# Gated cross-attention stack on one Trainium2 core: query projection and VectorE's rotation of it one step sooner in each batch of the first attention

## The chip, the cores and the metric

The kernel runs on one core of one Trainium2 chip. A core has TensorE (PE in the profile: matmuls, with weight loads shown apart as PEld), VectorE (DVE), ScalarE (ACT), GpSimd (POOL) and SyncE (SP, which here only issues transfers). The metric is the time of one execution in microseconds (us); lower is better.

## The reference

The program is four layers of attention and feed-forward over x, 16 batches of 128 rows and 256 columns, float32. The change touches the first attention of layer 0 alone. There the 128 rows of a batch are channels and the 256 columns are positions:

```
q = einsum('oc,bct->bot', Wq, layernorm(x)) + bq     # 16 heads of 8
k = einsum('oc,bct->bot', Wk, ctx) + bk              # 4 key heads of 8
v = einsum('oc,bct->bot', Wv, ctx) + bv
q = q * cos + rotate_half(q) * sin
k = k * cos + rotate_half(k) * sin
scores = einsum('bhqd,bhkd->bhqk', q, k) * scale     # 16 heads, 256 x 256
attn = softmax(scores, axis=-1)
out = einsum('bhqk,bhkd->bhqd', attn, v)
x = x + tanh(g) * (einsum('oc,bct->bot', Wo, out) + bo)
```

## The kernel before

Every engine runs a list of instructions written out by hand, and takes them in that order; semaphores tie the lists together. In the first attention (`l0_attention`) the lists of TensorE, VectorE, ScalarE and GpSimd all come from one loop over u = 0 to 127. Each u is a step; b = u // 8 is the batch and i = u % 8 the step in it, so a batch has 8 steps, called step 0 to step 7 below.

**What stands in every step.** TensorE computes a tile of scores (`pe_scores`, line 352, two matmuls into one of two score banks), then the scores of another batch once more with the row maximum taken off (`pe_shifted_scores`, line 374), then a second tile of scores. VectorE takes the row maximum of each tile of scores (`dve_max`, line 539), two per step. ScalarE takes the exponential of the shifted scores (`act_exp`, line 678). The maxima run 24 tiles (a batch and a half) ahead of the exponentials. A tile of scores may be written only when the maximum of the tile two before it has been taken:

```
pe.wait_ge(*maxed.at(v - 1))
```

**What stands in some steps.** These carry the batch b - 1 to its end and prepare the batch b + 3:

- Step 0: TensorE weighs the values with the exponentials, first half (`pe_weigh`, line 389, 16 matmuls); GpSimd normalises x of batch b + 3 (`pool_norm`, line 756), which the query projection reads.
- Step 1: TensorE turns the weighed values (`pe_turn_av`, line 397) and turns the context of batch b + 3 (lines 315, 316), which ScalarE copies (line 645); VectorE divides by the sums (`dve_normalise`, lines 562, 567).
- Step 2: TensorE weighs the second half (line 389 again).
- Step 3: TensorE turns it (line 397) and projects the queries of batch b + 3 (`pe_queries`, lines 322 and 323). VectorE splits the maxima of the batch b + 1 into three bfloat16 parts (`dve_split_top`, lines 547 to 553), divides (lines 562, 567) and rotates the queries (`dve_rope_queries`, lines 508 and 509, which read the bank of the projection). GpSimd adds the two halves of the rotation (line 761).
- Step 4: TensorE turns the split maxima (`pe_turn_top`, line 363), into the bank that the queries were in, so it waits for the split and for line 509:

```
pe.wait_ge(*top_split.at(b + 1))
...
elif b + 2 < NB:
    pe.wait_ge(*q_read.at(b + 3))
```

- Step 5: TensorE turns the outputs (line 403) and projects the keys (`pe_keys`, lines 330 and 331); VectorE rotates the keys (lines 519 and 520).
- Step 6: output projection (line 408), values of the context (lines 338 and 339), which VectorE copies with the bias (line 532).

The steps for batch b + 3 exist for b = 0 to 12, 13 times; the ones for b - 1 from b = 1. The query parts go to memory and come back as the stack that `pe_scores` of batch b + 3 reads, a batch and a half later.

Of the kernel before, what the change touches and what calls it, by code (L numbers as in the profile page):

```python
# [234 lines left out]
def l0_attention(m, l1):  # L235
# [75 lines left out]
    def pe_turn_context(b):  # L311
        pe.wait_ge(*ctx_in[b % 3].at(16 * (b // 3 + 1)))
        if b >= 3:
            pe.wait_ge(*v_ready.at(b))
        pe.transpose(k_bank(b)[:, 0:P], ctx_t[b % 3][:, 0:P], m.ident)
        pe.transpose(k_bank(b)[:, P:2 * P], ctx_t[b % 3][:, P:2 * P], m.ident).then_inc(*ctx_turned.up())

    def pe_queries(b):
        if b >= 3:
            pe.wait_ge(*ctx_kept.at(b + 1))  # L320
        pe.wait_ge(*xn_ready.at(b + 1))
        pe.matmul(q_bank(b)[:, 0:T0], wq, xn_t[b % 3], start=True, stop=True)
        pe.matmul(q_bank(b)[:, T0:2 * T0], wqp, xn_t[b % 3], start=True, stop=True).then_inc(*q_made.up())

    def pe_keys(b):
        if b >= 3:
            pe.wait_ge(*top_kept.at(b - 1))
        else:
            pe.wait_ge(*ctx_kept.at(b + 1))
        pe.matmul(k_bank(b)[0:32, 0:T0], wk[:, 0:32], ctx_t[b % 3], start=True, stop=True)  # L330
        pe.matmul(k_bank(b)[0:32, T0:2 * T0], wk[:, 32:64], ctx_t[b % 3], start=True, stop=True).then_inc(*k_made.up())

    def pe_values_of_context(b):
        if b >= 3:
            pe.wait_ge(*k_read.at(b + 1))
        else:
            pe.wait_ge(*q_read.at(b + 1))
        pe.matmul(q_bank(b)[:, 0:32], ctx_t[b % 3][:, 0:P], wv, start=True, stop=True)
        pe.matmul(q_bank(b)[:, 32:64], ctx_t[b % 3][:, P:2 * P], wv, start=True, stop=True).then_inc(*v_made.up())

    def pe_scores(v):
        b, hp, c = v // 16, v // 2 % 8, v % 2
        if v % 16 == 0:
            pe.wait_ge(*q_in[b % 3].at(16 * (b // 3 + 1)))
            pe.wait_ge(*k_in[b % 3].at(16 * (b // 3 + 1)))
        if v >= 2:
            pe.wait_ge(*maxed.at(v - 1))
        q3 = q_stack[b % 3].rearrange("p (h t) -> p h t", h=H0)
        k3 = k_stack[b % 3].rearrange("p (g t) -> p g t", g=G0)
        for j in range(2):  # L350
            h = 2 * hp + j
            last = pe.matmul(score_bank[v % 2][:, j * T0:(j + 1) * T0], q3[0:STACK + 48, h, c * P:(c + 1) * P], k3[0:STACK + 48, h // 4, :], start=True, stop=True)  # L352
        last.then_inc(*scored.up())

    def pe_turn_top(b):
        pe.wait_ge(*top_split.at(b + 1))
        if b == 0:
            pe.wait_ge(*v_ready.at(3))
        elif b + 2 < NB:
            pe.wait_ge(*q_read.at(b + 3))  # L360
        else:
            pe.wait_ge(*top_kept.at(b))
        pe.transpose(pro_bank.bitcast(BF16)[0:96, 0:P], top_part[b % 2], m.ident_bf).then_inc(*top_turned.up())
# [29 lines left out]
    def pe_turn_av(b, jp):  # L393
        n = 2 * b + jp
        pe.wait_ge(*av_kept.at(n + 1))
        for i in range(4):
            last = pe.transpose(av_bank[:, i * P:(i + 1) * P], av_t[jp][:, i * P:(i + 1) * P], m.ident)
        last.then_inc(*av_turned.up())
# [11 lines left out]
    def pe_program():  # L410
        pe_turn_context(0)
        pe.wait_ge(*w.q_loaded.now())
        pe_queries(0)
        pe.wait_ge(*w.k_loaded.now())
        pe_keys(0)
        pe_turn_context(1)
        pe_queries(1)
        pe_values_of_context(0)
        pe_keys(1)
        pe_turn_context(2)  # L420
        pe_queries(2)
        pe_values_of_context(1)
        pe_keys(2)
        pe_values_of_context(2)
        pe.wait_ge(*w.late.now())
        pe.wait_ge(*m.set_act.now())
        for v in range(AHEAD):
            pe_scores(v)
            if v == 16:
                pe_turn_top(0)  # L430
        for u in range(LAST):
            b, i = divmod(u, 8)
            v = 2 * u + AHEAD
            if v < NV:
                pe_scores(v)
            pe_shifted_scores(u)
            if v + 1 < NV:
                pe_scores(v + 1)
            if b >= 1:
                if i == 0:  # L440
                    pe_weigh(b - 1, 0)
                if i == 1:
                    pe_turn_av(b - 1, 0)
                if i == 2:
                    pe_weigh(b - 1, 1)
                if i == 3:
                    pe_turn_av(b - 1, 1)
                if i == 5:
                    pe_turn_out(b - 1)
                if i == 6:  # L450
                    pe_project(b - 1)
            if i == 4 and b + 1 < NB:
                pe_turn_top(b + 1)
            if b + 3 < NB:
                if i == 1:
                    pe_turn_context(b + 3)
                if i == 3:
                    pe_queries(b + 3)
                if i == 5:
                    pe_keys(b + 3)  # L460
                if i == 6:
                    pe_values_of_context(b + 3)
            if u == LAST - 8:
                pe.wait_ge(*m.l0f_weights.loaded.now())
            if u in (LAST - 8, LAST - 7):
                ffn.pe_turn_x(0, u - (LAST - 8))
            if u == LAST - 6:
                ffn.pe_router(0)
        last = NB - 1
        pe_weigh(last, 0)  # L470
        pe.wait_ge(*exped.at(LAST))
        ffn.pe_up(0)
        pe_turn_av(last, 0)
        pe_weigh(last, 1)
        ffn.pe_up(1)
        pe_turn_av(last, 1)
        pe_turn_out(last)
        pe_project(last)
# [91 lines left out]
    def dve_program():  # L570
        ffn.dve_clear()
        dve_clear_stack(0)
        dve_clear_stack(1)
        dve_clear_stack(2)
        dve_clear_values()
        for b in range(3):
            dve_norm_stats(b)
        for b in range(3):
            dve_norm(b)
        dve.wait_ge(*w.q_loaded.now())  # L580
        dve_rope_queries(0)
        dve.wait_ge(*w.k_loaded.now())
        dve_rope_keys(0)
        dve.wait_ge(*cleared.now())
        dve_rope_queries(1)
        dve_values(0)
        dve_rope_keys(1)
        dve_rope_queries(2)
        dve_values(1)
        dve_rope_keys(2)  # L590
        dve_values(2)
        dve.wait_ge(*m.set_act.now())
        dve.wait_ge(*w.late.now())
        dve.tensor_tensor(bo[:, 1:2], bo[:, 0:1], m.gates[:, 0:1], ALU.mult).then_inc(*cleared.up())
        for v in range(AHEAD):
            dve_max(v)
            if v == 15:
                dve_split_top(0)
        for u in range(LAST):
            b, i = divmod(u, 8)  # L600
            v = 2 * u + AHEAD
            if v < NV:
                dve_max(v)
            if v + 1 < NV:
                dve_max(v + 1)
            if i == 3 and b + 1 < NB:
                dve_split_top(b + 1)
            if b >= 1:
                if i == 1:
                    dve_normalise(b - 1, 0)  # L610
                if i == 3:
                    dve_normalise(b - 1, 1)
            if b + 3 < NB:
                if i == 0:
                    dve_norm_stats(b + 3)
                if i == 3:
                    dve_rope_queries(b + 3)
                if i == 5:
                    dve_rope_keys(b + 3)
                if i == 6:  # L620
                    dve_values(b + 3)
            if u == LAST - 12:
                for n in (0, 1):
                    dve.wait_ge(*q_out[n].now())
                    dve.wait_ge(*k_out[n].now())
                ffn.dve_set()
            if u == LAST - 11:
                ffn.dve_norm_stats(0)
            if u == LAST - 9:
                ffn.dve_norm(0)  # L630
            if u == LAST - 5:
                ffn.dve_router_logits(0)
            if u == LAST - 4:
                ffn.dve_router_top(0)
                ffn.dve_router_pick(0)
        dve_normalise(NB - 1, 0)
        ffn.dve_gate(0)
        dve_normalise(NB - 1, 1)
        ffn.dve_gate(1)
# [3890 lines left out]
```

## Time and profile before

| | |
|---|---|
| median of 3 runs | 1953.11 us (1948.66 to 1958.79) |
| profiled execution | 1949.41 us, its span 1948.1 us |
| busy: TensorE, VectorE, ScalarE, GpSimd | 87%, 68%, 49%, 41% of the span |
| mean granted clock of TensorE | 0.955 of full speed |
| VectorE row maxima, line 539 | 256, together 164.5 us |
| first attention, batches b = 1 to 12 | 58.69 to 263.56 us, about 17.07 us each |

An engine that is busy 87% of the span isn't busy so in every stage. What a change in one stage is worth is read from that stage: from the chain of work that ended last, and from what each engine waited for there.

### The profile page before, as it was taken

The page shows a single profiled execution, that of the slowest core. Times are in us where ns is not written, and L with a number is a line of the kernel's source. Part 1 is how long each engine was busy: PE and PEld are TensorE (multiplying, and loading weights), DVE is VectorE, ACT ScalarE, POOL GpSimd, SP SyncE. Part 2 cuts the span into 40 slices and gives each one's busy share as a digit, 9 for nine tenths or more (in the row PEclk, how much of TensorE's full clock was granted, in tenths as well). Part 3 has the DMA queues.
Part 4 walks back from the last instruction along what each step waited for, and adds up shares of the span by engine and source line. Part 5 has one row for each costly group of instructions (what it writes and reads, how often), then busy time and mean ns, then how long its engine had stood idle before and what let it go on. Part 6 is the DMA issues. An engine that isn't in the chain of part 4 may idle for free.

```text
span 1948.1 us, 35947 instructions
## 1 busy us (share of the span) xinstructions
PE 1702.4 (87%) x12191; PEld 1178.0 (60%) x12221; DVE 1327.5 (68%) x4195; ACT 945.2 (49%) x2227; POOL 789.6 (41%) x957
## 2 busy tenths in 40 slices
PE   6999988979897988989896787788999999987898
PEld 2444444646666777777684555456777777765445
DVE  7888874523466887887747888864667677667446
ACT  2767673213323777777544555334444444443352
POOL 3333321266654656664525454220143433343340
PEclk7999999989997999999898999799999999989898
DMA  4454422048843333443213543019010000031857
GB/s 110 103 124 104 97 54 90 23 157 304 287 138 84 85 88 84 95 84 68 74 37 102 154 120 82 17 37 322 1 36 19 33 10 1 13 98 37 240 192 307
DMA packets 180437, 200.41 MB, mean 103 GB/s; under 512 B 86500, under 2 KB 150129, under 8 KB 176928
## 3 DMA queue, kind: packets, MB, share of 16 engines
q1 hardware_dynamic: 164224, 156.32, 29.4%
q0 software_dynamic: 15168, 41.54, 6.2%
q8 instruction: 99, 1.62, 0.4%
q14 instruction: 82, 0.67, 0.1%
q10 hardware_dynamic: 864, 0.26, 0.1%
HBM read 131.88 MB, written 75.44 MB: 106 GB/s over the span
## 4 chain that ended last, share of the span: by engine, by line
PE 51%; DVE 24%; ACT 8%; issue 8%; POOL 4%; DMA 4%; SPq 1%; another core or an unknown queue 0%; DVEq 0%; ACTq 0%; POOLq 0%
PE psum L1058 4%; PE psum L3474 3%; PE psum L3400 3%; DVE sbuf L539 3%; PE psum L389 3%; PE psum L3449 2%; PE psum L352 2%; PE psum L3467 2%; PE psum L1337 2%; ACT sbuf L3837 2%; PE psum L2286 2%; PE psum L1070 2%; PE psum L1356 1%; PE psum L1702 1%; PE psum L4057 1%
## 5 line engine op out<-in xcount | busy, mean ns | idle before, releaser
L539 DVE TENSOR_REDUCE sbuf<-psum 128x2 f32<-128x512 f32 x256 | 164.5, 684 | 35.3 <-PE psum L352 34.2
L190 POOL TENSOR_TENSOR sbuf<-sbuf 128x1 f32<-128x1 f32 x128 | 73.2, 574 | 276.5 <-DVE sbuf L182 276.4
L2021 ACT ACTIVATE sbuf<-psum 128x512 f32<-128x512 f32 x256 | 137.8, 592 | 69.6 <-PE psum L1772 68.4
L3837 ACT ACTIVATE sbuf<-psum,sbuf 128x128 f32<-128x128 f32 x256 | 113.6, 455 | 89.8 <-DVE sbuf L3649 89.5
L678 ACT ACTIVATE sbuf<-psum 128x1024 f32<-128x1024 f32 x128 | 131.1, 1025 | 47.5 <-PE psum L374 43.1
L3929 POOL DMA_INDIRECT l_slot_inputs<-sbuf x96 | 97.0, 1011 | 102.0 <-DVE sbuf L3720 76.7
L3474 PE MATMUL psum<-sbuf 128*128 128x256 f32 x512 | 124.2, 386 | 4.9 <-DVE sbuf L3667 4.9
L352 PE MATMUL psum<-sbuf 112*128 112x256 bf16 x512 | 104.2, 288 | 16.3 <-DVE sbuf L539 11.2
L3400 PE MATMUL psum<-sbuf 128*128 128x256 f32 x512 | 117.0, 382 | 0.8 <-ACT sbuf L3801 0.8
L1897 DVE CUSTOM_DVE_ANT_0 sbuf<-psum,sbuf 128x128 f32<-128x128 f32 x512 | 112.6, 285 | 0.3 <-PE psum L1751 0.3
L3400 PEld LDWEIGHTS psum<-sbuf 128*128 128x128 f32 x512 | 97.1, 192 | 20.6 <-issue 8.6
L3474 PEld LDWEIGHTS psum<-sbuf 128*128 128x128 f32 x512 | 93.6, 193 | 16.1 <-issue 5.8
L352 PEld LDWEIGHTS psum<-sbuf 112*128 112x128 bf16 x512 | 41.8, 100 | 94.1 <-DVE sbuf L539 56.5
L1905 DVE TENSOR_REDUCE sbuf<-psum 128x8 f32<-128x1024 f32 x64 | 77.5, 1212 | 31.0 <-PE psum L1763 31.0
L1058 PE MATMUL psum<-sbuf 128*128 128x512 f32 (+1 forms) x192 | 86.7, 595 | 0.0
L2013 ACT ACTIVATE sbuf<-sbuf 128x128 f32<-128x128 f32 x256 | 81.3, 397 | 0.0
L3845 ACT ACTIVATE sbuf<-psum 128x512 f32<-128x512 f32 x64 | 38.4, 600 | 87.7 <-PE psum L3457 87.3
L3607 DVE COPY sbuf<-psum 128x1024 f32<-128x1024 f32 x32 | 39.2, 1224 | 60.3 <-ACT sbuf L3808 44.2
L3467 PE MATMUL psum<-sbuf 128*128 128x512 f32 x128 | 69.5, 625 | 9.8 <-ACT sbuf L3845 9.8
L3449 PEld LDWEIGHTS psum<-sbuf 128*128 128x128 f32 x512 | 67.3, 199 | 17.3 <-issue 15.1
L1772 PE MATMUL psum<-sbuf 128*128 128x128 f32 x512 | 68.5, 276 | 6.0 <-ACT sbuf L2021 5.8
L374 PE MATMUL psum<-sbuf 128*128 128x512 bf16 x226 | 70.7, 383 | 3.1 <-DMA sbuf<-sbuf 1.1
(436 smaller groups left out, 4474.0 us busy)
## 6 DMA issues: line engine op xcount, KB each, us to landing
l_pair_outputs<-sbuf SPq DMA_DIRECT2D x24, 512.0 KB, 7.1
sbuf<-in_l_gu_pairs SPq DMA_DIRECT2D x32, 384.0 KB, 8.1
sbuf<-l_pair_outputs SPq DMA_DIRECT2D x16, 768.0 KB, 15.9
sbuf<-l_q_parts SPq DMA_DIRECT2D x16, 384.0 KB
l_q_parts<-sbuf SPq DMA_DIRECT2D x64, 96.0 KB, 2.2
sbuf<-l_q_parts SPq DMA_DIRECT2D x32, 192.0 KB
l_k_parts<-sbuf SPq DMA_DIRECT2D x64, 96.0 KB, 2.1
sbuf<-l_k_parts SPq DMA_DIRECT2D x32, 192.0 KB
```

Of the source, the lines that this page charges most:

```text
L352: last = pe.matmul(score_bank[v % 2][:, j * T0:(j + 1) * T0], q3[0:STACK + 48, h, c * P:(c + 1) * P], k3[0:STACK + 48, h // 4, :], start=T ...
L539: dve.tensor_reduce(top3[:, 2 * hp:2 * hp + 2, c], score_bank[v % 2].rearrange("p (j t) -> p j t", j=2), AXX, ALU.max, negate=True).then_i ...
L678: act.activation(e_t[u % 12], shift_bank[u % 2], ACT.Exp).then_inc(*exped.up())
L1058: last = pe.matmul(up_bank[v % 2][0:M, n * BANK:(n + 1) * BANK], wn[:, k, fs], xt_t[blk][:, k, :], start=(k == 0), stop=(k == KD - 1))
L1897: last = dve.tensor_tensor_reduce(d_t[n % 3][:, head], self_bank[:, head], mask, -1.0, -LOWEST, ALU.add, ALU.min, mx[:, j:j + 1])
L2021: act.activation(e_t[i % 4][:, h * BANK:(h + 1) * BANK], turn_bank[:, h * BANK:(h + 1) * BANK], ACT.Exp).then_inc(*exped.up())
L3400: last = pe.matmul(q_bank[:, j * N:(j + 1) * N], w.wq[:, k, (4 * g + j) * P:(4 * g + j + 1) * P], xt_t[pair % 2][:, k, :], start=(k == 0), ...
L3449: last = pe.matmul(score_bank[:, j * P:(j + 1) * P], q[:, 4 * g + j, i * P:(i + 1) * P], kT_t[b % 3][:, g * P:(g + 1) * P], start=True, st ...
L3467: pe.matmul(av_bank, v_t[b % 3][:, g * P:(g + 1) * P], eT_t[u % 2], start=True, stop=True).then_inc(*valued.up())
L3474: last = pe.matmul(out_bank[:, 0:D], o_t[b % 2][:, h * P:(h + 1) * P], w.wo[:, h, :], start=(h == 0), stop=(h == H3 - 1))
L3837: last = act.activation(e_t[u % 3][:, j * P:(j + 1) * P], score_bank[:, j * P:(j + 1) * P], ACT.Exp, bias=mt[:, j:j + 1], scale=rq[:, lo + ...
L3929: pool.indirect_dma_start(out=route.x_slots[:, :], out_offset=bass.IndirectOffsetOnAxis(ap=route.slot[b][:, k:k + 1], axis=0), in_=xr_t[b ...
```

## The change

Two numbers in the loops change. `pe_queries(b + 3)` stands in step 2 of TensorE's list instead of step 3, and `dve_rope_queries(b + 3)` in step 2 of VectorE's list instead of step 3. No instruction is added or taken away. ScalarE's, GpSimd's and SyncE's lists are the same as before, among them GpSimd's addition (line 761) at its place of step 3.

```
@@ pe_program @@
                 if i == 1:
                     pe_turn_context(b + 3)
-                if i == 3:
+                if i == 2:
                     pe_queries(b + 3)
                 if i == 5:
                     pe_keys(b + 3)
@@ dve_program @@
                 if i == 0:
                     dve_norm_stats(b + 3)
-                if i == 3:
+                if i == 2:
                     dve_rope_queries(b + 3)
                 if i == 5:
                     dve_rope_keys(b + 3)
```

On TensorE, in batch b = 1 (and alike up to b = 12), the difference in the order is this; the first row is the last of the two score tiles of step 2, line 389 the weighing of step 2, lines 322 and 323 the query projection:

```order
 L352 MATMUL psum<-sbuf 128x256 x2
 L389 MATMUL psum<-sbuf 32x512 x8
-L352 MATMUL psum<-sbuf 128x256 x2
-L374 MATMUL psum<-sbuf 128x512 x2
-L352 MATMUL psum<-sbuf 128x256 x2
-L397 MATMUL psum<-sbuf 128x128 x4
 L322 MATMUL psum<-sbuf 128x256
 L323 MATMUL psum<-sbuf 128x256
+L352 MATMUL psum<-sbuf 128x256 x2
+L374 MATMUL psum<-sbuf 128x512 x2
+L352 MATMUL psum<-sbuf 128x256 x2
+L397 MATMUL psum<-sbuf 128x128 x4
```

The projection now stands directly behind the weighing, and ahead of the score tiles of step 3 and the turning behind them.

On VectorE, in the same batch, the four maxima of steps 2 and 3 (line 539) stood together before; lines 508 and 509 are the rotation. Its new place:

```order
-L539 TENSOR_REDUCE sbuf<-psum 128x2 x4
+L539 TENSOR_REDUCE sbuf<-psum 128x2 x2
+L508 SCALAR_TENSOR_TENSOR sbuf<-psum,sbuf 128x256
+L509 SCALAR_TENSOR_TENSOR sbuf<-psum,sbuf 128x256
+L539 TENSOR_REDUCE sbuf<-psum 128x2 x2
 L547 CAST sbuf<-sbuf 128x32
 L549 TENSOR_TENSOR sbuf<-sbuf 128x32
```

The rotation now stands between the two maxima of step 2 and the two of step 3, ahead of the split of the maxima. Its old place, some rows further on:

```order
 L562 RECIPROCAL sbuf<-psum 128x16
 L567 TENSOR_TENSOR sbuf<-psum,sbuf 128x4x16 x2
-L508 SCALAR_TENSOR_TENSOR sbuf<-psum,sbuf 128x256
-L509 SCALAR_TENSOR_TENSOR sbuf<-psum,sbuf 128x256
 L539 TENSOR_REDUCE sbuf<-psum 128x2 x4
```

Behind the division of step 3 the maxima of step 4 now follow at once.

## Rows read from the trace of the kernel before

**Rows 1.** Busy time by batch (x instructions), granted clock, DMA share and GB/s

```profile
58.69:75.76 17.07, 15.46 (x109) 8.31 (x115) 14.26 (x36) 11.97 (x19) 6.45 (x10) 1.00 0.51 121
...
246.49:263.56 17.07, 15.46 (x109) 8.31 (x115) 14.26 (x36) 11.97 (x19) 6.47 (x10) 1.00 0.39 91
...
278.55:298.35 19.80, 15.35 (x107) 6.82 (x113) 11.73 (x40) 13.41 (x18) 3.04 (x5) 1.00 0.02 6
```

**Rows 2.** Chain that ended last, 177.5 to 196 us: start, duration, engine, line

```profile
178.20 1.85 PE psum L389 x16
...
182.57 1.85 PE psum L389 x16
...
184.78 1.36 DVE sbuf L539 x2
...
188.36 0.61 DVE sbuf L539
...
190.28 0.55 PE psum L330 x2
...
195.26 0.97 PE psum L389 x5
```

**Rows 3.** Timeline, one batch: start, duration, engine, line, count [idle before, releaser]

```profile
180.69 1.23 POOL L756 TENSOR_SCALAR sbuf<-sbuf 128x256 f32<-128x256 f32 x1
...
182.23 1.28 DVE L539 TENSOR_REDUCE sbuf<-psum 128x2 f32<-128x512 f32 x2
...
182.50 1.92 PE L389 MATMUL psum<-sbuf 128*32 128x512 f32 x16
...
184.35 0.39 PE L352 MATMUL psum<-sbuf 112*128 112x256 bf16 x2
...
184.78 1.35 DVE L539 TENSOR_REDUCE sbuf<-psum 128x2 f32<-128x512 f32 x2 [1.27 <-PE psum L352]
...
185.57 0.30 PEld L322 LDWEIGHTS psum<-sbuf 128*128 128x128 f32 x2
185.68 0.60 PE L322 MATMUL psum<-sbuf 128*128 128x256 f32 x2
...
186.12 0.59 PE L323 MATMUL psum<-sbuf 128*128 128x256 f32 x2
186.17 0.18 DVE L547 CAST sbuf<-sbuf 128x32 bf16<-128x32 f32 x1
...
186.55 0.38 PE L352 MATMUL psum<-sbuf 112*128 112x256 bf16 x2
...
187.49 0.47 DVE L508 SCALAR_TENSOR_TENSOR sbuf<-psum,sbuf 128x256 f32<-128x256 f32 x1
...
188.28 2.52 DVE L539 TENSOR_REDUCE sbuf<-psum 128x2 f32<-128x512 f32 x4
...
188.50 0.23 PE L363 MATMUL psum<-sbuf 128*96 128x128 bf16 x1 [0.92 <-DVE sbuf L509]
...
189.01 0.39 PE L352 MATMUL psum<-sbuf 112*128 112x256 bf16 x2 [0.28 <-DVE sbuf L539]
...
190.22 0.62 PE L330 MATMUL psum<-sbuf 128*32 128x256 f32 x2
...
191.30 0.47 DVE L519 SCALAR_TENSOR_TENSOR sbuf<-psum,sbuf 32x256 f32<-32x256 f32 x1 [0.51 <-PE psum L331]
```

**Rows 4.** Who waited for whom, 40 to 400 us: total, times, longest

```profile
PE psum L363 <- DVE sbuf L509: 11.9, 13, 0.9
```

**Rows 5.** Timeline of the first batch, b = 0

```profile
46.61 3.71 DVE L539 TENSOR_REDUCE sbuf<-psum 128x2 f32<-128x512 f32 x6
...
47.43 1.23 POOL L756 TENSOR_SCALAR sbuf<-sbuf 128x256 f32<-128x256 f32 x1
...
50.36 0.18 DVE L547 CAST sbuf<-sbuf 128x32 bf16<-128x32 f32 x1
...
51.91 2.52 DVE L539 TENSOR_REDUCE sbuf<-psum 128x2 f32<-128x512 f32 x4
```

More of the change, by code:

```diff
@@ L456, in pe_program @@
                     pe_turn_context(b + 3)
-                if i == 3:
+                if i == 2:
                     pe_queries(b + 3)
@@ L615, in dve_program @@
                     dve_norm_stats(b + 3)
-                if i == 3:
+                if i == 2:
                     dve_rope_queries(b + 3)
```

## The prediction

> **What bounds the kernel now.** I read the stage first, then its chain, then the waits at the two places that move. The busy time by batch shows that the twelve batches b = 1 to 12 are the same batch over and over: 17.07 us, TensorE busy 15.46 of it, VectorE 14.26, clock at full speed [rows 1]. No engine is full, so the length of a batch is set by a path that goes to and fro between engines. The chain that ended last runs through this stage, and it comes back to the same place after a batch: line 389 at 178.20 and again at 195.26 [rows 2]. Between them it goes from the second weighing on TensorE (step 2, 182.57) to VectorE's two maxima of step 3 (184.78), stays on VectorE until the first maximum of step 4 (188.36), goes to TensorE's score tiles and key projection of step 5 (190.28), and round again. Since the chain closes on itself in each batch, whatever is added between two of its points is added to every batch, and what is taken off elsewhere counts nothing.
>
> Both moved pieces lie between its points at 182.57 and 188.36. The timeline shows this stretch closely [rows 3]. The weighing of step 2 holds TensorE until the score tile of step 3 starts at 184.35. VectorE has finished the maxima of step 2 at 182.23 + 1.28 = 183.51 and stands idle for 1.27 us until that tile is there, at 184.78. It then takes the two maxima (1.35), the split of the maxima from 186.17, the division, the rotation of the queries from 187.49 and, with no gap, the first maximum of step 4 at 188.28.
>
> Two waits invite the change. One is VectorE's idle 1.27 us. The other is TensorE's 0.92 us ahead of line 363 in step 4, put down to line 509, the end of the rotation [rows 3]; it comes in all 13 batches and sums to 11.9 us [rows 4].
>
> **The change part by part.** I lay out the stretch anew, with the durations of these rows, from the point 184.35 where the weighing lets TensorE go. Nothing ahead of this point changes.
>
> *The projection on TensorE.* It stands directly behind the weighing. Its inputs are there: GpSimd's normalised x ends at 180.69 + 1.23 = 181.92 [rows 3]. So it starts at 184.35. From the start of its first matmul to VectorE's first reading there are two nearby rows. The key projection, also four matmuls over 256 columns that start behind a gap, goes from 190.22 to VectorE's start at 191.30, which is 1.08 us; the query projection itself goes from 185.68 to the end of line 323 at 186.12 + 0.59 = 186.71, which is 1.03 us [rows 3]. I take 1.08, the one with the handover in it: the rotation can start at 184.35 + 1.08 = 185.43.
>
> *The idle of VectorE is not where the rotation goes.* The 1.27 us end at 184.78, and the rotation's input is there only at 185.43. VectorE waits for it 0.65 us beyond the end of the old gap. Behind the waiting rotation the two maxima of step 3 are queued, and for those wait the split, the division and the maxima of step 4. The rotation takes 188.28 - 187.49 = 0.79 us, so it ends at 186.22.
>
> *The score tiles of step 3* are 186.55 - 185.68 = 0.87 us later on TensorE, about 185.2 instead of 184.35. The first is ready after 0.43 us (184.35 to 184.78), at about 185.65, before 186.22: this delay lies under the rotation. The second tile is written about 0.67 us behind the first (an estimate: two matmuls of line 374 lie between them) and is ready at about 186.3; its maximum starts only at 186.85. So both maxima run back to back.
>
> *The maxima, split and division.* Before, from the first maximum to the split, 186.17 - 184.78 = 1.39 us. Where the four maxima of steps 4 and 5 run with all tiles ready they take 2.52 / 4 = 0.63 us each, 1.26 the two [rows 3]. I take 1.32, between the two; the bounds are 1.26 and 1.39. The split starts at 186.22 + 1.32 = 187.54. From the split to the end of the division there are 187.49 - 186.17 = 1.32 us, unchanged, and the rotation is no longer behind it. The first maximum of step 4 thus starts at 188.86, and not at 188.28: **0.58 us later in each batch**. The same in short: 0.65 of new wait, less 0.07 on the pair. With the bounds (maxima 1.26 to 1.39; projection 1.03 to 1.19, the upper end if its first weight load, 185.57 to 185.68 in these rows, isn't hidden: 1.08 + 0.11) it is 0.47 to 0.76.
>
> *TensorE's wait in step 4.* The 0.92 us ahead of line 363 shrink: it now waits for the split alone, at about 188.4. But directly behind stands the score tile of step 5 (189.01), which waits for the first maximum of step 4; it was idle another 0.28 us for it, after line 363 was through [rows 3]. That maximum now ends 0.58 later, so the tile starts at about 189.6. The wait of line 363 is given back to the wait behind it and is worth nothing. Its cover is the maximum; without that it would be worth up to 0.92.
>
> *Everything else.* GpSimd's addition, ScalarE's first part and the transfers of the query parts keep their places in lists that did not change; their input is there sooner and nobody on the chain waits for them. They stand queued behind other work in step 4 as before. They are costed at nothing.
>
> *The first batch, b = 0*, has no weighing and no division. Six maxima run from 46.61 to 50.32; four of them, those of steps 1 and 2, end at 46.61 + 4 x 3.71 / 6 = 49.08 [rows 5]. The projection needs GpSimd's x, ready at 47.43 + 1.23 = 48.66. With 1.08 the rotation can start at 49.74, so VectorE waits 0.66 us that it did not wait before. This batch costs +0.66 (0 to 0.8).
>
> *Sum*: 12 x 0.58 + 0.66 = 7.6 us. The batches 13 to 15 hold no projection. What follows, the router and the experts of layer 0, starts from the end of this chain, so I carry the sum whole. The profiled execution took 1949.41 us, 1.3 more than its span of 1948.1; changed it would take 1957.0. The median of the three runs is 3.70 above the profiled execution, and I place the forecast on the median: 1953.11 + 7.6 = **1960.7 us**, +0.39%.
>
> *A rule to weigh.* The rows say that VectorE takes its list strictly in order: the rotation's input was ready at 186.71, and it started only at 187.49, behind the split and the division [rows 3]. The Trainium skill, "PSUM — Partial Sum Buffer", section "Engine vs sequencer instructions", says that the queues of VectorE, ScalarE and GpSimd are strict FIFO and that matmuls start in program order; by this rule the waiting rotation stops the maxima behind it, and the trace agrees. Were it otherwise, the maxima of step 3 would go first, at about 185.65, and the rotation would follow on them: 185.65 - 184.78 = 0.87 a batch in place of 0.58, so the forecast would be 1953.11 + 11 = 1964.
>
> **The rivals.**
> - *Line 363 decides (faster).* If TensorE's 0.92 us in step 4 were on the path, the change would free it 13 times: up to 11.9 us [rows 4], 1941.2. It decides only if the first maximum of step 4 ends before 188.50; it ends at 188.36 + 0.61 = 188.97 [rows 2], and the chain does not pass through line 363. Against it too: that maximum moves later.
> - *The gap takes it (faster).* If the rotation fell into the idle 1.27 us it would leave the path, 0.79 x 13 = 10.3 us, 1942.8. It would need its input by 184.78 - 0.79 = 183.99, and the weighing ahead of it on TensorE ends at 184.35. Excluded by the order unless the weighing starts 1.4 us sooner. The two together 4 in 100.
> - *Absorbed (no change).* VectorE is idle 0.51 us ahead of the key rotation in step 5 [rows 3] and could take the delay there. But this idle ends with the key projection (190.28), which is itself on the chain behind the delayed maximum [rows 2]. If half of the delay went there, 1957; if all, 1953. 12 in 100.
> - *A slower clock (slower).* The batch gets longer with the same work, 15.46 of 17.65 us, 88%. If the granted clock fell for a part of the stage, each half-speed batch would cost several us and the sum would pass 1970. The last window of the stage has TensorE busy only 15.35 of 19.80, 78%, with the clock at 1.00 [rows 1], so 88% should hold it. 4 in 100.
> - *A longer handover (slower).* Both upper bounds: 12 x 0.76 + 0.8 = 9.9, 1963. Or the maxima slowed by TensorE writing the score banks at another time than before. 15 in 100.
>
> **How the numbers follow.** The forecast itself has 65 in 100. With the low bounds, 12 x 0.47 + 0 = 5.6, and the high ones, 9.9, it gives 1958.7 to 1963.0 on this median. The three runs spread from 1948.66 to 1958.79, so a new median may lie some 3 us to either side; the range is 1955 to 1967, which also takes in half of the absorbed case. About 0.5% (9.8 us) is what a measurement of this kernel can tell from no change; the forecast of +0.39% lies under it, and only the handover and clock rivals, and the spread around the sum, go over it: slower 0.28, within 0.69, faster 0.03.
>
> **What would show it.** In the changed trace: batches of 17.65 us instead of 17.07; line 508 directly behind the maxima of step 2 with an idle of about 1.9 us ahead of it, put down to line 323; no idle ahead of the maxima of step 3; the wait of line 363 much shorter and put down to line 553, and a longer one of the score tile of step 5 behind it; the chain going from line 389 over lines 322, 323, 508 to 539. The prediction is wrong if the batch keeps 17.07 us or gets shorter, if the rotation starts before 185.3 in this batch's own time, or if the time goes elsewhere than into steps 2 to 4.

## The result and the profile after

The changed kernel takes 1964.4 us (median of 13 runs), the kernel before 1948.7 us beside it (13 runs): a ratio of 1.0074, 95% interval 1.0052 to 1.0096. It is slower, and the interval is clear of no change. The ratio leaves out one of the changed kernel's 13 executions as slow (1977.6 us, mean granted clock 0.943). Run again on another chip it gave 1969.5 against 1953.1 us, 1.0091 (1.0058 to 1.0124). The forecast was +7.6 us, +0.39%; the sign and the range held, the size was about half of what was measured.

First the batch, between two weighings of step 0, in the busy time by batch of the changed kernel (columns as in [rows 1]):

```profile
58.45:76.20 17.75, 15.86 (x108) 8.37 (x108) 14.21 (x36) 11.77 (x19) 6.46 (x10) 1.00 0.48 116
...
182.70:200.45 17.75, 15.86 (x108) 8.36 (x108) 14.21 (x36) 11.76 (x19) 6.48 (x10) 1.00 0.43 95
```

A batch is 17.75 us and not 17.07 [rows 1]: 0.68 us more, where 0.58 was forecast.

The timeline of one batch, to be read against [rows 3]:

```profile
187.07 1.92 PE L389 MATMUL psum<-sbuf 128*32 128x512 f32 x16
...
188.93 0.70 PE L322 MATMUL psum<-sbuf 128*128 128x256 f32 x2
...
189.89 0.38 PE L352 MATMUL psum<-sbuf 112*128 112x256 bf16 x2
...
190.09 0.48 DVE L508 SCALAR_TENSOR_TENSOR sbuf<-psum,sbuf 128x256 f32<-128x256 f32 x1 [2.00 <-PE psum L323]
...
190.89 1.28 DVE L539 TENSOR_REDUCE sbuf<-psum 128x2 f32<-128x512 f32 x2
...
192.20 0.18 DVE L547 CAST sbuf<-sbuf 128x32 bf16<-128x32 f32 x1
...
193.10 0.26 PE L363 MATMUL psum<-sbuf 128*96 128x128 bf16 x1 [0.35 <-DVE sbuf L553]
...
193.53 2.52 DVE L539 TENSOR_REDUCE sbuf<-psum 128x2 f32<-128x512 f32 x4
...
194.27 0.39 PE L352 MATMUL psum<-sbuf 112*128 112x256 bf16 x2 [0.90 <-DVE sbuf L539]
...
196.56 0.47 DVE L519 SCALAR_TENSOR_TENSOR sbuf<-psum,sbuf 32x256 f32<-32x256 f32 x1 [0.51 <-PE psum L331]
```

VectorE now stands idle for 2.00 us ahead of the rotation, until the end of line 323; the maxima of step 3 follow the rotation with no gap. From the end of the weighing's hold on TensorE to the first maximum of step 4 it is 193.53 - 188.93 = 4.60 us; before it was 188.28 - 184.35 = 3.93 [rows 3]. Line 363 waits only 0.35 us instead of 0.92, and the score tile behind it 0.90 instead of 0.28: one wait went into the other.

Who waited for whom, over the eleven batches from 75.76 to 263.56 us:

```profile
DVE sbuf L508 <- PE psum L323: 22.1, 11, 2.0
...
PE psum L352 <- DVE sbuf L539: 15.7, 31, 0.9
...
PE psum L363 <- DVE sbuf L553: 3.6, 10, 0.4
```

Twelve such batches are 12 x 0.68 = 8.2 us. The first batch is 0.9 us longer: from its maxima of step 1 to the first maximum of step 4 it is 51.75 - 45.53 = 6.22 us, and before it was 51.91 - 46.61 = 5.30 [rows 5]. That is 9.1 of the 15.7 us between the two profiled executions (1965.1 and 1949.4). The first batch of the changed kernel:

```profile
45.53 2.52 DVE L539 TENSOR_REDUCE sbuf<-psum 128x2 f32<-128x512 f32 x4
...
51.75 2.52 DVE L539 TENSOR_REDUCE sbuf<-psum 128x2 f32<-128x512 f32 x4
```

In this profile the granted clock is 1.00 in all twelve batches, so the rest lies behind them. Batch 15, the last one, from its first weighing to the next, in the changed kernel and in the kernel before:

```profile
299.71:317.78 18.07, 13.59 (x84) 7.22 (x83) 8.19 (x47) 11.06 (x16) 3.68 (x6) 0.90 0.00 0
```

```profile
291.75:308.21 16.46, 11.95 (x82) 6.07 (x83) 8.19 (x47) 10.73 (x16) 3.67 (x6) 1.00 0.00 0
```

The clock falls here for a short time (0.90 in the mean of the batch), which costs 1.6 us, and a second fall right behind costs as much. The last output projection of this attention ends at 334.6 us, and before at 323.4: 11.2 us later, made up of 9.1 + 3.2 less 1.1 by which this execution had reached its first batch sooner. The other 4.5 us come behind the stage; between 800 and 1300 us the mean granted clock is 0.91, and before it was 0.93. One pair of executions cannot tell how much of this is scatter, so where the rest of the loss lies was left to the experiments.

### The profile page after: what moved, and what is told of

It reads as the page before. It is cut to its first block and busy times, and to the rows that moved or that the text cites. A ratio compares the mean times of both kernels' runs of the same rounds, so it can differ in the third digit from the quotient of the medians.

```text
span 1963.8 us, 35977 instructions
## 1 busy us (share of the span) xinstructions
PE 1717.9 (87%) x12221; PEld 1181.8 (60%) x12221; DVE 1327.6 (68%) x4195; ACT 944.5 (48%) x2227; POOL 791.8 (40%) x957
## 5 line engine op out<-in xcount | busy, mean ns | idle before, releaser
L374 PE MATMUL psum<-sbuf 128*128 128x512 bf16 x256 | 77.8, 385 | 0.9 <-DMA sbuf<-sbuf 0.6
```

## The experiments

Whole kernels are compared with the kernel before on the same chip, interval in brackets. The chips differ by about 1% (the kernel before had medians of 1953 us beside the first four rows and 1936 us beside the fifth), so whole kernels are compared by their ratios alone. To see the stage without the scatter of all that follows, several kernels were cut off behind the first attention; they compute no more than that and are compared with each other. The first four cut kernels below ran on one chip and the last three on another, where the whole kernel before had medians of 1933.6 and 1933.8 us; so their times are compared as they stand. The cut kernel before was not run on the second chip.

| kernel | time, us | against |
|---|---|---|
| change again | 1969.5 | 1.0091 (1.0058 to 1.0124) |
| projection alone moved | 1974.7 | 1.0120 (1.0086 to 1.0154) |
| rotation longer, nothing moved | 1957.9 | 1.0028 (1.0006 to 1.0049) |
| projection ahead of the weighing | 1955.8 | 1.0012 (0.9991 to 1.0032) |
| division later | 1933.0 | 0.9991 (0.9963 to 1.0020) |
| cut: before | 336.2 (335.7 to 339.2) | |
| cut: change | 348.2 (344.6 to 353.1) | +12.0; +11.1 without the longest of the five |
| cut: rotation longer | 349.1 (347.1 to 349.5) | +12.9 |
| cut: projection alone moved | 358.4 (357.2 to 358.7) | +22.2 |
| cut: change, TensorE's idle filled | 344.6 (343.6 to 347.7) | +8.4 |
| cut: division later | 333.3 (331.1 to 333.9) | -2.9 |
| cut: rotation alone moved | 381.5 (377.4 to 382.0) | +45.3 |

**The change once more.**

> The changed kernel once more, as a ruler for the runs beside it. Its batch of the stage was 17.75 us in the trace (17.07 before), 12 x 0.68 = 8.2 us, but its time was 14 us above the kernel before. Theory A (the stage is all of the change, the rest of the difference was the drift of single executions): ratio near 1.0042. Theory B (the later stages also lose, because the changed kernel reaches them at another time and TensorE's clock is granted less): ratio 1.006 to 1.009 and a mean granted clock below that of the kernel before.

It gave 1.0091, and a mean granted clock of 0.949 over its executions where the kernel before beside it had 0.952 (both are means over the runs' clocks). The chance of single executions is not the cause; theory B stays, as far as "the clock is granted less" goes. Whether in later stages is another matter.

**The projection alone.**

```
@@ pe_program @@
-                if i == 3:
+                if i == 2:
                     pe_queries(b + 3)
```

> The projection alone in step 2, the rotation stays in step 3. Path theory: TensorE takes the projection (0.96 us in the changed trace, 188.93 to 189.89) ahead of the score tiles of step 3, VectorE's two maxima and all behind them start that much later, and the rotation stays on VectorE's path: batch 17.07 + 0.9 to 1.0 = about 18.0 us, +11 in the stage, so worse than the whole change. Rival (the wait of the rotation is what costs, and the projection on TensorE is free): batch 17.1 us, no change.

The batch is 18.03 us in the profile, +0.96, as the path says; the rival, a free projection, is out. But 12 x 0.96 = 11.5 us stand against a ratio of 1.0120, about 23 us (17 to 30).

**A longer rotation, nothing moved.**

```
@@ dve_rope_queries @@
+        if b >= 3:
+            dve.scalar_tensor_tensor(q_a, q_bank(b)[:, 0:T0], bq[:, 0:1], cosq, ALU.add, ALU.mult).then_inc(*m.chain.up())
+            dve.wait_ge(*m.chain.now())
         dve.scalar_tensor_tensor(q_a, q_bank(b)[:, 0:T0], bq[:, 0:1], cosq, ALU.add, ALU.mult)
```

> The order of the kernel before, with the first instruction of the query rotation done one time more in each of the 13 batches (0.39 us and a handover of about 0.23). Nothing is moved; this only lengthens VectorE's path. Path theory: batch 17.07 + 0.62 = 17.7 us, +8 us in the stage, as much as the change. Theory A: total +8, ratio 1.004. Theory B (any shift of the later stages by some 8 us costs more there): total +12 to +16, ratio 1.006 to 1.008.

The batch is 17.60 us, +0.53. The ratio, 1.0028, looks like theory A: no more than the stage's own 12 x 0.53 = 6.4 us. A shift of the later stages by itself costs nothing that can be seen here. The cut version below makes this less simple.

**The projection ahead of the weighing.**

```
@@ pe_program @@
             if b >= 1:
+                if i == 2 and b + 3 < NB:
+                    pe_queries(b + 3)
                 if i == 2:
                     pe_weigh(b - 1, 1)
...
-                if i == 2:
+                if i == 2 and b == 0:
                     pe_queries(b + 3)
```

> Rotation in step 2 as in the changed kernel, but the projection ahead of the weighing of step 2 on TensorE (in b = 0, where there is no weighing, as in the changed kernel). Path theory: the rotation's input is there about 1.1 us after 182.5 in the time of the trace before, at 183.6, so the rotation falls into VectorE's idle time, 183.6 to 184.4; the weighing and the tiles of step 3 are 0.87 us later (maxima from 185.65 instead of 184.78) but the rotation's 0.79 is off the path: batch 17.07 + 0.08, 17.1 to 17.3 us, no change in the total within 2 us. Rival (the place of the rotation ahead of the maxima is the cost by itself): batch stays near 17.7.

Here the rotation does fall into VectorE's idle time. The profile is of the longest of its 13 executions, but its batches have the clock at 1.00. The busy time of the batch and VectorE's timeline (line numbers of this kernel are 2 higher, so 510 is the rotation, 541 the maxima, 549 the split):

```profile
61.60:78.76 17.16, 15.55 (x108) 8.32 (x108) 14.33 (x36) 11.75 (x19) 6.47 (x10) 1.00 0.49 120
```

```profile
65.71 1.28 DVE L541 TENSOR_REDUCE sbuf<-psum 128x2 f32<-128x512 f32 x2
66.95 0.48 DVE L510 SCALAR_TENSOR_TENSOR sbuf<-psum,sbuf 128x256 f32<-128x256 f32 x1
67.35 0.47 DVE L511 SCALAR_TENSOR_TENSOR sbuf<-psum,sbuf 128x256 f32<-128x256 f32 x1
69.13 1.35 DVE L541 TENSOR_REDUCE sbuf<-psum 128x2 f32<-128x512 f32 x2 [1.30 <-PE psum L352]
70.51 0.18 DVE L549 CAST sbuf<-sbuf 128x32 bf16<-128x32 f32 x1
```

The rotation starts behind the maxima of step 2 without any wait, and the batch is 17.16 us, +0.09 where 0.08 was worked out. The place of the rotation costs nothing by itself; what costs is that its input comes behind the weighing. It gains nothing either: the rotation's 0.79 us are off VectorE's path, the projection's 0.87 are on TensorE's. TensorE's waits in steps 4 and 5 are those of the changed kernel, 0.35 and 0.90 us:

```profile
105.72 0.26 PE L363 MATMUL psum<-sbuf 128*96 128x128 bf16 x1 [0.35 <-DVE sbuf L555]
106.88 0.39 PE L352 MATMUL psum<-sbuf 112*128 112x256 bf16 x2 [0.90 <-DVE sbuf L541]
```

**The stage by itself.** The same cut in all of them: the remaining programs are left out, and x goes out as it stands behind the first attention.

```
@@ l0_attention, program @@
     pool_program()
-    ffn.program()
...
+    sp.wait_ge(*m.x_l0a.at(NB))
+    for b in range(NB):
+        sp.dma_start(m.out[b], m.X[b]).then_inc(*stored.up(16))
```

> The kernel before, cut off behind the first attention: the feed-forward of layer 0 (but for the pieces of it that stand in the attention's own lists) and the layers 1 to 3 are left out, and x as it then is goes out. Its time is a ruler for the three kernels beside it: about 320 us to the last output projection, and 8 to 15 us for the store, 330 to 340 us.

> The changed kernel, cut off in the same way. The whole changed kernel was some 15 us slower than before, and the batches explain 12 x 0.68 + 0.3 = 8.5. Theory C (the rest arises in this stage, as TensorE's clock falls in it for some executions, where it stayed full in the profile before): 12 to 17 us above the cut kernel before, a wider spread of the executions and a lower mean clock. Theory D (the rest arises in later stages): 8 to 9.5 us above it, with the same clock.

> The order of before with the first instruction of the rotation done once more, cut off in the same way. Its batch was 17.60 us in the trace, so 12 x 0.53 + about 0.6 = 7.0 us by the path. Theory C in its narrow form (the order of the changed kernel lets the clock fall, not the longer batch): 7 us above the cut kernel before. In its wide form (any longer batch does): 9 us or more.

> The projection alone moved, cut off in the same way. Its batch was 18.03 us in the trace, so 12 x 0.96 + about 1 = 12.5 us by the path. Its profile showed six short falls of the clock in the stage, some 37.6 us apart, and the whole kernel was 22 us slower. Theory C: 17 to 22 us above the cut kernel before; Theory D: 12 to 14.

All three are further above the cut kernel before than their path: 12.0 against 9.1, 12.9 against 7.0, 22.2 against 12.5 us. So losses beyond the path do arise in this stage (theory C), and in its wide form: the longer rotation, which moves nothing, has them too. For the change itself the evidence is weaker than for the other two: without its longest execution it is 11.1 us, between the 8 to 9.5 of theory D and the 12 to 17 of theory C. The ratio 1.0074 makes 14 us on 1948.7 (10 to 19 by its interval), so the stage holds most of that, and some may lie behind it.

What it is, the busy time by batch shows. The cut kernel before, two batches:

```profile
98.15:115.22 17.07, 15.58 (x109) 8.32 (x108) 14.27 (x36) 11.98 (x19) 6.48 (x9) 1.00 0.46 115
115.22:132.29 17.07, 15.58 (x109) 8.32 (x108) 14.27 (x36) 11.97 (x19) 6.48 (x9) 1.00 0.50 120
```

The cut kernel with the projection alone moved, four:

```profile
82.83:102.29 19.46, 17.25 (x109) 8.85 (x108) 14.47 (x36) 11.88 (x19) 6.49 (x9) 0.91 0.43 104
102.29:120.31 18.02, 15.66 (x108) 8.41 (x107) 14.26 (x36) 11.96 (x19) 6.49 (x9) 1.00 0.46 115
120.31:139.75 19.44, 17.24 (x108) 8.82 (x107) 14.49 (x36) 11.87 (x19) 6.47 (x9) 0.91 0.42 98
139.75:157.78 18.03, 15.83 (x108) 8.37 (x107) 14.27 (x36) 11.97 (x19) 6.47 (x9) 1.00 0.54 133
```

The cut changed kernel, three, and with the longer rotation, two:

```profile
100.33:118.08 17.75, 15.86 (x108) 8.37 (x107) 14.21 (x36) 11.76 (x19) 6.49 (x9) 1.00 0.43 112
118.08:137.42 19.34, 17.45 (x109) 8.99 (x108) 14.36 (x36) 11.76 (x19) 6.48 (x9) 0.91 0.42 106
137.42:155.17 17.75, 15.86 (x109) 8.38 (x108) 14.21 (x36) 11.76 (x19) 6.48 (x9) 1.00 0.50 129
```

```profile
99.45:117.04 17.59, 15.58 (x109) 8.32 (x108) 14.76 (x37) 11.99 (x19) 6.49 (x9) 1.00 0.44 112
117.04:136.05 19.01, 17.16 (x108) 8.68 (x108) 14.98 (x37) 11.87 (x19) 6.47 (x9) 0.91 0.42 103
```

The third number from the end, 1.00 or 0.91, is the granted clock. Some batches have it at 0.91, and each of these is 1.4 to 1.6 us longer than its neighbours. With the projection alone moved it is every second batch: from the first weighing of b = 1 (60.44) to that of b = 13 (285.29) the profile has 224.9 us, 12 x 18.03 = 216.4 and 8.5 over, for six such batches 1.42 each. With the longer rotation it has 215.4, 4.3 over 12 x 17.59, for three. The cut changed kernel has 279.80 - 60.46 = 219.3, 6.3 over 12 x 17.75, for four. The profile of the cut kernel before has none: 264.46 - 59.63 = 204.8, 12 x 17.07; but one of its five executions took 339.2 us at a mean clock of 0.940, so it need not be free of falls in all of them.

That profile of the cut changed kernel is of the longest of its executions. The whole changed kernel shows the same kind of batch, once in the profile of its second run, shown here, and not at all in the first profile above:

```profile
113.02:132.39 19.37, 17.20 (x106) 8.92 (x108) 14.35 (x36) 11.74 (x19) 6.47 (x10) 0.91 0.43 105
```

The timeline of TensorE in such a batch of the cut changed kernel shows what a fall of the clock is and what comes ahead of it. The last line is the busy time of the stretch:

```profile
124.12 0.26 PE L363 MATMUL psum<-sbuf 128*96 128x128 bf16 x1 [0.36 <-DVE sbuf L553]
125.28 0.61 PE L352 MATMUL psum<-sbuf 112*128 112x256 bf16 x2 [0.90 <-DVE sbuf L539]
125.68 1.06 PE L374 MATMUL psum<-sbuf 128*128 128x512 bf16 x2
126.54 0.64 PE L352 MATMUL psum<-sbuf 112*128 112x256 bf16 x2
126.96 0.63 PE L403 MATMUL psum<-sbuf 128*128 128x128 f32 x2
127.53 1.06 PE L330 MATMUL psum<-sbuf 128*32 128x256 f32 x2
128.38 0.74 PE L331 MATMUL psum<-sbuf 128*32 128x256 f32 x2
129.06 0.39 PE L352 MATMUL psum<-sbuf 112*128 112x256 bf16 x2
```

```profile
125.28:128.66 3.38, 3.38 (x11) 1.71 (x12) 1.93 (x3) 1.60 (x3) 0.73 (x2) 0.50 0.24 66
```

Right behind the two waits of step 4 and 5, 0.36 and 0.90 us, TensorE runs at its lower level, 1.2 GHz (granted clock 0.50): the pair of line 374 takes 1.06 us instead of 0.60, the key projection 1.06 instead of 0.62 [rows 3]. At 129.06 it is back at 2.4 GHz.

These two waits stand in every batch of this order, also in the eight of the same profile and the twelve of the first profile that have no fall, so they alone do not bring it. With the projection alone moved the falls come behind one long wait:

```profile
89.80 0.23 PE L363 MATMUL psum<-sbuf 128*96 128x128 bf16 x1 [1.79 <-DVE sbuf L509]
90.31 0.39 PE L352 MATMUL psum<-sbuf 112*128 112x256 bf16 x2 [0.28 <-DVE sbuf L539]
```

What sorts the kernels is how long TensorE waits in steps 4 and 5 in sum. The table has all profiles of this stage, those of the three experiments below among them:

| kernel | TensorE's waits in steps 4 and 5, us | batches with a fall, of 12 |
|---|---|---|
| division later, whole and cut | 0.37 + 0.28 | 0, 0 |
| cut: change, TensorE's idle filled | 0.34 + 0.59 | 0 |
| before, whole and cut | 0.92 + 0.28 | 0, 0 |
| projection ahead of the weighing | 0.35 + 0.90 | 0 |
| change: first profile, again, cut | 0.34 + 0.36 + 0.90 | 0, 1, 4 |
| rotation longer, whole and cut | 1.44 + 0.28 | 3, 3 |
| projection alone moved, whole and cut | 1.79 + 0.28 | 6, 6 |
| cut: rotation alone moved | 1.66 + 0.36 + 0.90 | 12 |

This is an order among eight kernels, one execution to a profile. It does not say why one batch has a fall and the next, with the same waits, has none.

**TensorE's idle filled.** If the fall comes from idle time, work that nobody needs should make the kernel faster.

```
@@ pe_program @@
+            if i == 4 and b + 3 < NB:
+                pe.wait_ge(*q_read.at(b + 4))
+                for _ in range(2):
+                    pe.matmul(pro_bank[:, 0:T0], wq, xn_t[b % 3], start=True, stop=True)
             if i == 4 and b + 1 < NB:
                 pe_turn_top(b + 1)
```

> The changed kernel cut off behind the first attention, with two more copies of the first query matmul (four instructions, about 0.9 us) on TensorE ahead of line 363 in step 4, into the bank that it overwrites; nobody reads them. TensorE stands idle there and behind it for 0.35 + 0.90 us in the changed trace, so they should not lengthen the batch: 17.75 us still. Theory C (what the batches don't explain is the clock falling because TensorE idles too much): the falls go, granted clock 1.00 in every window of the stage, time 336.2 + 8.5 = 344.7 us with a small spread, against 348.2 for the cut changed kernel. If the falls have another cause: 348 us and more, with windows of 0.91.

344.6 us, where 344.7 was written down, and 3.6 less than without the added matmuls (2.7 less if the longest execution without them is left out). Busy time of one batch, and of 20 us behind the last of them:

```profile
164.70:182.45 17.75, 16.52 (x113) 9.05 (x112) 14.21 (x36) 11.87 (x19) 6.49 (x10) 1.00 0.42 95
```

```profile
300.00:320.00 20.00, 15.48 (x100) 7.08 (x93) 7.83 (x45) 10.88 (x17) 3.67 (x6) 0.91 0.00 1
```

The batch is still 17.75 us, TensorE is busy 16.52 of it and not 15.86, and the clock is at 1.00 in all windows from 60 to 300 us. It falls only behind them, from 300 us on, where nothing was filled in. The executions of the two kernels overlap (343.6, 344.5, 344.6, 347.5, 347.7 against 344.6, 346.4, 348.2, 349.1, 353.1), and the two upper ones of the filled kernel have a lower mean clock, 0.941 and 0.942 against 0.952 to 0.954: some falls remain in some executions, and whether in the batches or behind them their clocks do not tell. Nor does the one profile decide it, since the first profile of the changed kernel has no fall in its batches either. That the filling takes the falls away is therefore likely, and not shown.

**The rotation alone.**

```
@@ dve_program @@
-                if i == 3:
+                if i == 2:
                     dve_rope_queries(b + 3)
```

> The rotation alone in step 2, the projection stays in step 3, cut off in the same way. Path theory: the rotation waits until the projection of step 3 is through, 186.71 in the time of the trace before, then 0.79, the maxima of step 3 behind it 1.32, split and division 1.32: first maximum of step 4 at 190.2 instead of 188.28, batch 19.0 us, 12 x 1.9 = 23 us and about 1.5 in b = 0, 361 us with a full clock; with falls of the clock as in the other longer batches 365 to 375. Rival (order does not bind, the maxima overtake the waiting rotation): batch under 18 us, 350 us or less.

It came out at 381.5 us, above the upper end of 375. VectorE waits 3.23 us ahead of the rotation, and every batch has a fall; VectorE's timeline and the busy time:

```profile
167.82 1.28 DVE L539 TENSOR_REDUCE sbuf<-psum 128x2 f32<-128x512 f32 x2
172.33 0.48 DVE L508 SCALAR_TENSOR_TENSOR sbuf<-psum,sbuf 128x256 f32<-128x256 f32 x1 [3.23 <-PE psum L323]
```

```profile
61.14:81.71 20.57, 17.36 (x108) 8.87 (x108) 14.35 (x36) 11.75 (x19) 6.44 (x10) 0.92 0.41 100
81.71:102.28 20.57, 17.36 (x112) 8.92 (x113) 14.40 (x36) 11.79 (x19) 6.52 (x10) 0.92 0.41 100
```

20.57 us is the expected 19.0 and one fall of 1.6. The maxima do not overtake the waiting rotation.

**A version to beat both: the second division later.**

```
@@ dve_program @@
-                if i == 3:
+                if i == 4:
                     dve_normalise(b - 1, 1)
```

> The order of before, cut off in the same way, with the second division (lines 562, 567) of each batch moved from step 3 to step 4, behind the two maxima. By the path it leaves the stretch from the split to the first maximum of step 4 (0.55 us less there), and the outputs' turning and key projection wait a little for it, about 0.2: batch 16.7 us, 12 x 0.37 = 4.4 us less, 331.8 us, if the clock stays full. If the shorter batch lets the clock fall as the longer ones did: 334 to 338 us.

> The whole kernel in the order of before, with the second division of each batch moved from step 3 to step 4. Cut off behind the first attention it was 333.3 against 336.2 us, with a batch of 16.83 us. The path carries the 2.9 us to the end: ratio 0.9985, 0.9965 to 1.0005, which this measurement may not tell from no change. Rival (the shift alone costs later stages their clock): ratio above 1.001.

The batch is 16.83 us with the clock at 1.00, 0.24 less than before and not 0.37, and the cut kernel is 2.9 us faster. That 12 x 0.24 is 2.9 too is in part chance: this execution started its batches 1.3 us sooner than that of the cut kernel before, and has one fall behind them. The batch:

```profile
62.70:79.53 16.83, 15.79 (x108) 8.27 (x107) 14.22 (x36) 11.87 (x19) 6.49 (x9) 1.00 0.52 125
```

The whole kernel gave 0.9991 (0.9963 to 1.0020). That fits a gain of 2.9 us in 1936 and shows none: it beats the changed kernel, and the kernel before only in the cut version (no execution in common: 331.1 to 333.9 against 335.7 to 339.2 us, on two chips).

## Why the prediction was right in its direction and short in its size

- **The range held in part by luck.** It stood on 1953.11 us, the median of three executions. The kernel before had 1948.7 over the 13 beside the changed kernel, 4.4 lower; on that base the range would have been 1951 to 1963 us, and 1964.4 lies above it. What was measured is +15.8 us where +7.6 was forecast.
- **The chain and where the change meets it**: right. The batch got longer by what lies between the weighing of step 2 and the first maximum of step 4, and by nothing else.
- **The idle of VectorE is not where the rotation goes**: right, and shown from both sides. With the projection behind the weighing VectorE waits 2.00 us (1.92 forecast); with it ahead of the weighing the rotation starts with no wait.
- **The handover**: 1.08 us was taken; it is 190.09 - 188.93 = 1.16, near the upper bound of 1.19. The first of these matmuls takes 0.70 us behind the weighing, not 0.60.
- **The pair of maxima**: 1.32 taken, 192.20 - 190.89 = 1.31 measured. From the split to the first maximum of step 4 it is 1.33, where 1.32 was taken. The sum, 4.60 against 3.93, gives 0.67; the batch shows 0.68, the forecast 0.58 with an upper bound of 0.76. The first batch, 0.66 forecast with an upper bound of 0.8, is 0.9 longer. The path as a whole is 9.1 us and not 7.6.
- **The wait of line 363 given back**: right. 0.92 became 0.35 and the wait behind it went from 0.28 to 0.90. Rivals one and two, the faster ones, are out, and so is "absorbed": the 0.51 us of VectorE in step 5 stayed.
- **Strict order on VectorE**: right. With the rotation alone moved, three microseconds of waiting held the maxima.
- **"I carry the sum whole"**: not borne out. Of the 15.7 us between the two profiled executions 9.1 are the path, and 3.2 are two falls of the clock behind the twelve batches, where the forecast has no term.
- **The step that failed is the rival "a slower clock"**, which had 4 in 100. Its ground was that the last window of the stage held 1.00 with TensorE busy 78%, "so 88% should hold it". The mean of a long window said nothing about it: among batches at 89% (15.86 of 17.75) some have falls and some have none. Its price was wrong too. Not several us a batch and a sum past 1970, but 1.4 to 1.6 us a fall, in a part of the batches or behind them. Together with the path it makes the 12.0 us of the cut kernel: 9.1 and about two falls.
- **The chances**: "within 0.5%" had 0.69 since the sum was 7.6 us against a bound of 9.8. With the 0.10 us a batch more and the falls it is 11 to 12 in the stage, over the bound.

What is shown and what is not. That the batch is longer since VectorE waits for the projection behind the weighing is shown, by the kernels that move one piece alone and by the one that puts the projection ahead. That falls of the clock make the difference between path and time in this stage is shown where the profiles count them: 8.5 us for six with the projection alone moved, 4.3 for three with the longer rotation. For the changed kernel three profiles have none, one and four in the batches, so their share in its loss differs from execution to execution. That TensorE's waits bring the falls fits the order of the eight kernels and the lower median of the filled one, and is not shown. The Trainium skill, "TensorE: Matmul & The Clock Gate", section "What's actually happening", says that the default state is the throttled one and that activity releases it; the filled kernel points the same way, its median 3.6 us lower with the matmuls added in each batch, but its executions overlap with those of the kernel without them.

Open: the longer rotation costs 12.9 us in the cut kernel, but 1.0028 (1.0006 to 1.0049) as a whole, 5.5 us, at most 9.6. For the changed kernel stage and whole agree within their scatter. Somewhere behind the stage the one got back what the other did not, or the falls in the stage, which differ from execution to execution, were fewer in the whole kernel's other executions (its profile, of the second longest of twelve, had three falls and a first attention 12 us longer than before). No run here tells these apart. The kernels' mean clocks over all executions, 0.953 for the longer rotation and 0.949 for the change, do not say in which stage the clock was lower. Open too is what decides which batch has a fall.

## What to carry to other kernels

An idle time on one engine can take a piece of work only if that work's input is there by its beginning; here the input was made by the engine for which the idle one was waiting, behind the same long piece, so the move turned 1.3 us of idle into 2.0. Where a path goes round between engines once per batch, price a move by the stretch between two fixed points of that path, and then look at TensorE's clock in several executions, since it can cost most of the path again: with the projection alone moved the path was 12.5 us and the falls and the rest 9.7 more. The stage cut out of the kernel told a difference of 3 us apart, where the whole kernel's interval was 11 us wide.

## What the hardware showed that was not expected

- TensorE's clock falls to its lower level for a short stretch with the engine busy 89% of the batch (15.86 of 17.75 us before the fall) and no single wait above 0.90 us around it; in the other orders of the stage the longest wait ahead of a fall is 1.79 us. A batch with a fall is 1.4 to 1.6 us longer.
- Batches with the same waits have a fall or none. In the eight kernels of the table the count goes up with TensorE's waits in steps 4 and 5, from none of twelve batches over every second one to all twelve.
- With matmuls whose result nobody reads the stage had the lower median, 344.6 instead of 348.2 us, with executions that overlap.
